# A four-layer conditioned network on one core: layer 1's adapters mixed on GpSimd, the prologue chain and PE's order changed, the last part's products stacked

## The reference

```python
for l in range(4):
    x = x + ffn_l(cond_l(x, cond_512))

# cond_l: four times
s = style @ mw.T + mb
weight = SCALE * w * s[:, None, :, None]
demod = lax.rsqrt(jnp.sum(weight * weight, axis=(2, 3)) + EPS)
out = conv(x, weight * demod) + b        # same, upsample + blur, same, blur + downsample

# ffn_1
A_eff = einsum('bn,nri->bri', gate, lora_A)      # gate 8 x 16, lora_A 16 x 32 x 1024
B_eff = einsum('bn,nor->bor', gate, lora_B)      # lora_B 16 x 1024 x 32
out = x @ kernel + bias + (x A_eff^T) B_eff^T + (x A_s^T) B_s^T

# ffn_3: H = x W^T + b, z = x A
logits = 0.5 * H_slice / max|H_slice| + 0.5 * (z LiMEs^T) / max|z LiMEs^T|    # odd positions
weights = normalised softmax with a soft top-2 mask
out = H + 0.5 * (z * (weights LiMEs)) Bmat
```

## Time and profile before

| | us |
|---|---|
| median of 3 runs | 2082.81 (2082.38 to 2083.69) |
| profiled execution | 2085.02 |
| its span, first to last instruction | 2083.3 |
| PE busy | 1893.3 |
| DVE busy | 905.4 |
| ACT busy | 646.3 |
| POOL busy | 82.7 |

### The profile page before, as it was taken

How to read it: one execution, slowest core, us unless ns; L and a number is a source line. 1 busy time by engine, 2 the same in 40 slices (tenths; PEclk the granted TensorE clock), 3 DMA queues, 4 the chain that set the end, 5 groups by cost and what they waited for, 6 DMA issues and landing times.

```text
span 2083.3 us, 28693 instructions
## 1 busy us (share of the span) xinstructions
PE 1893.3 (91%) x9806; PEld 1563.2 (75%) x9806; DVE 905.4 (43%) x2634; ACT 646.3 (31%) x1169; POOL 82.7 (4%) x140
## 2 busy tenths in 40 slices
PE   3789999869999999985799999999879999999978
PEld 2567777757888888864688888888767888888855
DVE  5345555644343433344434444444563333333244
ACT  0045555423333333314322232332153332233200
POOL 0000000000000000000000000000000000000000
PEclk9999999969999999986899999999989999999975
DMA  6256666423223323235222222222233232222226
GB/s 125 56 108 149 148 158 155 104 60 82 69 76 82 83 74 83 58 67 119 59 69 58 70 68 58 70 68 52 86 80 79 68 78 66 70 70 78 58 91 262
DMA packets 248777, 182.99 MB, mean 88 GB/s; under 512 B 197688, under 2 KB 207960, under 8 KB 248734
## 3 DMA queue, kind: packets, MB, share of 16 engines
q1 hardware_dynamic: 242750, 175.07, 33.1%
q0 software_dynamic: 4496, 2.12, 1.0%
q10 hardware_dynamic: 1488, 5.26, 0.8%
HBM read 108.99 MB, written 44.04 MB: 73 GB/s over the span
## 4 chain that ended last, share of the span: by engine, by line
PE 75%; issue 9%; DVE 7%; DMA 4%; SPq 4%; ACT 1%; DVEq 0%; POOL 0%; ACTq 0%; POOLq 0%
PE ps L812 61%; PE ps L1485 4%; PE ps L891 3%; DMA filt<-filt 2%; PE ps L939 2%; DVE w_lo L1240 2%; SPq L1073 1%; DMA out_x<-raw 1%; SPq L1310 1%; PE ps L882 1%; DMA raw<-in_x 1%; PE ps L1353 1%; PE ps L1359 1%; SPq L1306 1%; DVE filt L650 1%
## 5 line engine op out<-in xcount | busy, mean ns | idle before, releaser
L812 PE MATMUL ps<-xp_hi,filt 128*128 128x512 f32 x1024 | 338.9, 413 | 28.1 <-DMA filt<-filt 27.9
L812 PE MATMUL ps<-w_hi,y_hi 128*128 128x512 f32 x768 | 313.6, 408 | 0.0
L812 PE MATMUL ps<-w_hi,y_lo 128*128 128x512 f32 x768 | 306.6, 399 | 0.0
L812 PE MATMUL ps<-w_lo,y_hi 128*128 128x512 f32 x768 | 306.3, 399 | 0.0
L812 PEld LDWEIGHTS ps<-xp_hi,filt 128*128 128x128 f32 x1024 | 192.1, 195 | 71.5 <-DMA filt<-filt 30.3
L639 DVE SCALAR_TENSOR_TENSOR xp_lo<-ps,mods_pair,xp_hi 128x512 fp32r<-128x512 f32 x128 | 96.3, 753 | 268.9 <-ACT xp_hi L391 268.9
L812 PE MATMUL ps<-xp_lo,filt 128*128 128x512 f32 x512 | 205.8, 402 | 0.0
L391 ACT ACTIVATE xp_hi<-ps,mods_pair 128x512 fp32r<-128x512 f32 x128 | 88.4, 691 | 359.4 <-PE ps L812 359.4
L812 PEld LDWEIGHTS ps<-w_lo,y_hi 128*128 128x128 f32 x768 | 146.0, 190 | 35.6
L812 PEld LDWEIGHTS ps<-w_hi,y_hi 128*128 128x128 f32 x768 | 147.7, 192 | 31.5
L812 PEld LDWEIGHTS ps<-w_hi,y_lo 128*128 128x128 f32 x768 | 146.6, 191 | 31.1
(11 more groups left out here) (315 smaller groups left out, 3212.3 us busy)
## 6 DMA issues: line engine op xcount, KB each, us to landing
x_in<-x_state SPq DMA_DIRECT2D x96, 256.0 KB, 3.9
x_res<-x_state SPq DMA_DIRECT2D x48, 512.0 KB, 4.0
x_state<-x_res SPq DMA_DIRECT2D x48, 512.0 KB, 2.9
filt<-filt SPq DMA_DIRECT2D x128, 128.0 KB, 2.7
filt<-filt SPq DMA_DIRECT2D x128, 96.0 KB, 2.4
raw<-in_x SPq DMA_DIRECT2D x16, 512.0 KB, 5.0
x_res<-in_x SPq DMA_DIRECT2D x16, 512.0 KB, 3.9
x_state<-raw SPq DMA_DIRECT2D x16, 512.0 KB, 2.9
```

The source lines that it names most:

```text
L812: ins = nc.tensor.matmul(out, st[x0], mv[x1], start=first and t == 0, stop=last and t == 2, **kw)
```

## The change

**Mixing.** `mix_loads`, `mix_dve`, `mix_pe` and the store on SP go. POOL loads the 16 A and 16 B adapters one by one in their natural layout (two buffers), multiplies each with the gate, broadcast over all partitions, and adds it to an accumulator, in two halves of four samples. `mix_pool` is called for four adapters behind each edge load of layer 0; then POOL stores the result. In layer 1, `load_mixed` (SP) reads one group's mixture in that natural layout, `pe_mixed` transposes it on PE (ten transposes, ahead of the tail of each odd step), `act_mixed` and `dve_mixed` bring it into place.

**Prologue.** The clearing of buffers moves from DVE to POOL. The squared weights are made first and have a semaphore of their own; PE transposes them and mod_w and makes the modulation and the norms before it transposes the convolution forms. ACT, in layer 0, copies the transposed forms. x of pair 0 is loaded ahead of layer 0's adapters, x of pair 1 ahead of the filter's shift. Layer 0's adapters are transposed after the halves of pair 1. In layers 0 and 1 the edge stages lie between halves and first products.

**PE's order.** The second filter is built before the convolution of pair 0. In the steps of layers 1 to 3 the projection stands ahead of the halves and edge stage 2, and edge stage 1 behind the convolution.

**Last part.** hi and lo of z and Bmat are stacked on 96 partitions (z_hi, z_lo, z_hi against B_hi, B_hi, B_lo), so each pair takes one matmul per half instead of three. The weights are transposed in one product and multiplied with LiMEs laid out by pair (`limes_of`). Bmat and LiMEs are made ready during the last steps of layer 3. The last two pairs stay in SBUF and aren't stored to the state; the other 14 are read back into 14 buffers, and the sums are written in place over them, each stored from there.

The core of the diff:

```diff
@@ PE, steps of layers 1 to 3
+            if l == 1 and j == 0:
+                pe.wait_ge(s["mixed_proj"], i + 1)
+            if one_more:
+                pe_conv(pe, l, n + 1, 1)
+            if l == 1 and j == 0:
+                pe.wait_ge(s["mixed_dve"], i + 1)
             if edges:
                 pe_edge(pe, l, i + 1, 1)
+            pe.wait_ge(s["dve_t"], smp(l - 1, n, 1))
+            if l in (1, 3):
+                pe.wait_ge(s["act_f"], whole_y(l, n, 1))
             if one_more:
-                pe_conv(pe, l, n + 1, 1)
+                pe.wait_ge(s["act_y"], smp(l, n + 1, 1))
...
+            pe_project(pe, l, i, j)
             if edges:
                 pe.wait_ge(s["dve_e"], edge_count(l, i + 1, 4))
...
-            pe_project(pe, l, i, j)
@@ the mixing
+        def mix_pool(gp, k):
+            m, n = divmod(k, 16)
+            gp.wait_ge(mix_loaded[k % 2], 16 * (k // 2 + 1))
+            done = mix_count(k)
             for half in range(2):
+                acc = mix_a[:, 4 * half:4 * half + 4] if m == 0 else (mix_b0, mix_b1)[half][:]
+                src = mix_in[:, k % 2].unsqueeze(1).to_broadcast([P, 4, 256])
+                gate = gate_bc[:, 4 * half:4 * half + 4, n].unsqueeze(2).to_broadcast([P, 4, 256])
...
+                gp.wait_ge(s["mix_ops"], done)
+                gp.tensor_tensor(mix_tmp[:], src, gate, ALU.mult).then_inc(s["mix_ops"], 1)
+                gp.wait_ge(s["mix_ops"], done + 1)
+                gp.tensor_tensor(acc, acc, mix_tmp[:], ALU.add).then_inc(s["mix_ops"], 1)
+                done += 2
+            if k + 2 < 32:
+                gp.wait_ge(s["mix_ops"], done)
+                load_adapter(gp, k + 2)
...
+        def pe_mixed(pe, g, bank):
+            pe.wait_ge(s["mixed_loaded"], 16 * (g + 1))
+            for h in range(2):
+                nc.tensor.transpose(ps[:, bank, P * h:P * h + P], nat_mix[:, 0, h:256:2], ident[:])
+            for o in range(8):
+                last = nc.tensor.transpose(ps[0:32, 2 + 2 * (o % 2), o // 2:512:4], nat_mix[:, 1, 32 * o:32 * o + 32], ident[:])
+            last.then_inc(s["mixed_pe"], 1)
@@ the last part
-                    last = mm3(ps[:, 2 * (n % 2) + h, :], [t[:, P * n:P * n + P] for t in (zp_hi, zp_lo)],
-                               [t[:, M * h:M * h + M] for t in (bm_hi, bm_lo)], True, True)
+                    last = mm(ps[:, 2 * (n % 2) + h, :], zp_st[:, P * n:P * n + P], bm_st[:, M * h:M * h + M], start=True, stop=True)
...
+            sp.wait_ge(s["pe_o"], pid(LAYERS, 0))
+            for n in range(HELD):
+                sp.dma_start(x_last[:, n], xs_rows[n]).then_inc(fin_loaded[n], 16)
             for n in range(PAIRS):
                 sp.wait_ge(s["fin_x"], n + 1)
+                sp.dma_start(out_rows[n], held_out(n)).then_inc(s["fin_stored"], 16)
@@ POOL's queue
+            for g in range(1, GROUPS):
+                pool_load_edge(gp, 0, g)
+                for k in range(4 * g - 4, 4 * g):
+                    mix_pool(gp, k)
+            load_cond_rest(gp, 1)
+            for k in range(4 * GROUPS - 4, 4 * GROUPS):
+                mix_pool(gp, k)
+            mix_store(gp)
@@ PE, start of a layer
                 pe_filter(pe, l, 0)
                 pe_halves(pe, l, 1)
+                if l == 0:
+                    pe.wait_ge(s["dve_p"], smp(0, 0, 1))
+                    pe.wait_ge(s["dve_e"], edge_count(0, 0, EDGE_OPS))
+                    ffn_pe_prep(pe, 0)
+                pe.wait_ge(s["dve_k"], smp(l, 0, 1))
+                pe_filter(pe, l, 1)
...
                 pe_conv(pe, l, 0, 0)
                 pe_conv(pe, l, 0, 1)
```

More of the change, by code:

```diff
@@ L45 @@
 EDGE_OPS = 10
-X_LAST = 6
+HELD = 14
 PROJ_W = (136, 64, 252, 32)
@@ L789, in dve_step @@
                 dve_tail_in(dve, l, n)
+            if not more and j == 0 and l + 1 == LAYERS:
+                held_ready_dve(dve)
             if nxt and j == 0:
@@ L1604, in final_act, with held_out @@
+            weigh(0)
+            weigh(1)
+            lower(0)
+            lower(1)
+            add(0)
+            add(1)
+            weigh(2)
+            add(2)
+            lower(2)
+            weigh(3)
+            add(3)
+            lower(3)
+            for n in range(4, PAIRS):
+                add(n)
+        def held_out(n):
+            return x_last[:, n - 2] if n > 1 else raw[:, n]
         def final_act(act):
-            act.wait_ge(s["pe_o"], pid(LAYERS, 0))
-            nc.scalar.activation(natural(bm_hi[:]), tail_raw[0:32].rearrange("p (m h) -> p m h", h=2), ACT.Copy,
-                                 scale=0.5).then_inc(s["bm_act"], 1)
```

583 lines of the change are left out of this document (338 added, 245 removed).

## The result

The changed kernel takes **2175.3 us** (median of 4 runs, 2171.5 to 2179.4), the kernel before 2082.8: a ratio of 1.044, with a 95% interval of 1.042 to 1.046. It is slower by 92.5 us where 60 us less were forecast. The profiled execution has a span of 2177.7 us.

A forecast was written before the change was run, and what follows sets the result against it. PE, busy 91% of the span, was taken as the bound. Terms -62.5 + 0 + 9 + 30 - 6 - 31 = -60.5 us turn the 2082.8 us median into 2022; 8-in-10 range 1990 to 2085.

The forecast's parts named there:

- Mixing on POOL ... 0 us: Layer 0: POOL's 124 multiplies and adds, 2.4 us each (p), barely fit beside the loop and cost 0 us.
- Rival 2: Layer 0: DVE instructions with two SBUF inputs wait for POOL operations, +88 us, time 2110; one chance in seven.
- Prologue chain: Conditioning chain before layer 0: bias products end about 30.4 instead of 39.97; gain 9.6 us, bounds 6 and 11.
- From there to the first convolution: After the chain, 40.8 us instead of 93.7; layer 0's first loop convolution at 71.2, -62.5 us including the chain.
- Layer 1's transposes: Layer 1 loop: ten more transposes on PE per group, 1.25 us each group, +9 us for seven groups.
- Projection ahead of the halves: Layers 1 to 3: PE waits for y_nat, 1.03 us in odd steps, 0.25 in most even ones; +30 us.
- Starts: Starts of layers 1 to 3: waits for the filter shift and fb_lo go, -2 us each; -6 us in all.
- Last part: After layer 3's last matmul: fewer matmuls and no waits for stores, over near 2052; -31 us, bounds -26 and -33.

The follow-up runs named there:

- Runs 2 and 6: Changed kernel: 2, each of GpSimd's 120 multiplies and adds replaced by two memsets, 2069.5 us; 6, two small VectorE copies written as reductions, 2164.0 us.
- run 4: Changed kernel with the last four adapters mixed on GpSimd before its wait for layer 0's last filter: 2164.3 us.
- run 7: Changed kernel with GpSimd operations in four pieces, last four adapters mixed before the wait, and old TensorE order in layers 1 to 3: 2097.2 us.

## Why the prediction was wrong, point by point

**The step that failed: "Mixing on POOL ... 0 us".** Its own numbers were good, though they were scaled from a different instruction, the affine_select: the multiply took 1.95 us and the add 2.45. An adapter of four operations with its load takes 9.7 to 10.7 us (loads at 202.35, 213.03 and 222.68), so p is 2.3 to 2.5 with its wait, against 2.4; a group of layer 0 holds 54.9 - 13.9 = 41.0 us of POOL work, against 42.1. POOL was never the bound: it waits 12.4 to 17.8 us for `e_x` in every group. The error was to ask only whether POOL fits in the time, and not what it does to its neighbour. Price: 127 us between the medians (131 between the profiled executions), for a term of 0.

**Rival 2 was the answer, at one chance in seven, and still too cheap.** It gave DVE as the bound at 44 us and a group of 50; measured are 41.9 us of DVE's own time (167.58 of 215 us) and 53.8. That its price of a group came so near was luck. It gave 23 us a group to the instructions with two SBUF inputs, which in fact grew by 9.4 (`gu_lo`, `x_lo`, `w_lo`, `e_h`, `e_z`; their means less those of before), and it left out copies, casts and `tensor_scalar`, which grew by 11.5: `y_nat`, `mods_pair`, `xp_hi` from `end_hi`, `end_hi` and `e_y`, with `y_nat` alone 21.9 - 2.7 = 19 us in four groups. And it priced only the seven groups: 17.6 us in the prologue and 23.2 at the end of layer 0 came on top. The Trainium skill, page "SBUF — State Buffer", section "Who interferes with whom", had all of it: copies, casts and `tensor_scalar` can run in a mode that takes both ways in, and then exclude GpSimd; an instruction with two SBUF inputs contends only with a GpSimd instruction that reads SBUF; and a reduction never contends. Runs 2 and 6 agree with each of the three (0.79, 0.42 and 0.15 us). The prediction quoted the half of the rule on two inputs.

**The queue behind the wait was missed.** The budget let POOL be done at 376 and had `load_cond_rest` as a matter of three issues. It is a wait until layer 0's last filter, in front of a group's worth of mixing. The step "each queue that it is moved past" was not carried out for it. It cost 11 us (run 4). With the slower pieces DVE stood 56 us for these loads (run 7), and issuing them from SP gave back 38.6 (2097.2 to 2058.6).

**Prologue chain: right.** The last bias product ends at 30.3 in the kernel after, 30.4 forecast. (The 39.97 that it takes for the end of the last memset is its start; that is 0.06 us.) Inside the chain the norms end 2 us late (21.8 instead of 19.8), and the bias products make up for it: they start at 27.3 and take 3.1 us.

**From there to the first convolution: mis-sized by 9.** It was to be near 71; without POOL's operations it starts at 80.2, with them at 85.4. The narrow transposes took 7 us and their split 4.4, as forecast; in the run without the operations the stretch from edges to filter took 20.5 instead of 13.8. The forecast let three of the four waits for DVE vanish behind PE's work, while DVE's chain runs at its own pace: PE still waits 4.1 us in three places, 2.2 of them for `x_lo`. And the twelve first products and fifteen filter matmuls took 9.1 us instead of the old 5.3 (0.63 and 0.41 us each against 0.39 and 0.28), though the granted clock of that stretch (39 to 51 us) reads 1.00; why is open. Later the convolution took 7.2 instead of 6.2, and two waits of 1.3 us together stood before the transposes.

**Layer 1's transposes: right.** 7.7 us for seven groups, 9 forecast.

**Projection ahead of the halves: right.** The wait is 0.96 us in odd steps and 0.16 in even ones (1.03 and 0.25 forecast), worth 35.3 and 32.7 us in two pairs of runs against the 30 forecast. Of that the waits in the three loops are some 26 us (8.5 each); the rest is stretches of lower clock and later starts of layers 2 and 3, which were not in it.

**Starts: layer 1 wrong, layer 2 right in most runs, layer 3 wrong.** Layer 1 starts 7.9 us later instead of 2 sooner. DVE in the run without operations and with the old order:

```profile
386.34 0.91 DVE L1313 MEMSET tail_raw<- 32x1024 f32 x1 [0.15 <-issue]
...
390.67 2.04 DVE L1318 TENSOR_TENSOR tail_lo<-tail_raw,tail_hi 65x1024 fp32r<-65x1024 f32 x1 [2.12 <-ACT tail_hi L1298]
```

The base split moved from the loop to the start and stands ahead of the first `e_x`: 0.91 + 2.12 + 2.04 = 5.1 us, with PE waiting (7.5 us instead of 2.4). The gain in the loop was counted, and its new place was not. The wait of 4.0 us for the shifted filter did go, as forecast, but a wait of 2.5 us for `filt` came in beside the 1.9 for `fb_lo`, and only the latter had been allowed for. PE is also busy 7.0 us longer there (70.1 of 88 us against 63.1 of 77, granted clock 0.78 against 0.84). Layers 2 and 3 start 2.4 and 2.1 us sooner in that run (113.7 and 84.9 against 116.1 and 87.0 from pair 15 to pair 0), as forecast. But for layer 3 this is the exception: in the other five runs with the old order it takes 88.0 to 88.1, 1 us more than before, and in the changed kernel 5 us more. Layer 2 takes 113.7 to 114.0 in four of these six runs and 117.0 and 117.3 in two.

**Last part: right.** 49.3 us from the last residual addition, 30.0 less than before (31 forecast); the first of its sixteen additions starts 22.0 us behind it. The stretch that answers to the last of the earlier trace rows:

```profile
2160.00:2170.00 10.00, 8.89 (x16) 4.00 (x16) 9.02 (x9) 0.00 (x0) 0.00 (x0) 0.50 0.98 388
```

DVE is busy 9.02 of 10 us there, against 4.23 before, with PE at the lower of its clock levels in both.

**Left open.** Why the granted clock falls in some steps and not in others like them, and how the 5 us at the start of layer 3 divide between waits and clock. A mixing whose products are made on ScalarE, with half the work on GpSimd, wasn't tried.

## What to carry over

Moving work to GpSimd is not free because GpSimd was idle: list VectorE's instructions that run beside it, by form. In these runs those with two SBUF inputs waited out a running GpSimd instruction that read SBUF, and copies and casts within SBUF even one that only wrote; the profile books this as their own busy time. If the work must go there, make each GpSimd instruction short (in four pieces: 2175 to 2101 us) while GpSimd itself has time to spare, and look in its queue for the wait that the moved work now stands behind, or that stands behind it.
